# Cross-attention kernel: the first steps of each quad of heads in another order

## What is computed

```python
x = x + _L0_xattn_ref(_layernorm(x, axis=-1), ctx_2048, Wq, Wk, Wv, Wo)
# H, HD = 16, 128; 4096 keys
q = (inputs_q @ Wq).reshape(b, sq, H, HD) * (1.0 / np.sqrt(HD))
k = (inputs_kv @ Wk).reshape(b, skv, H, HD)
v = (inputs_kv @ Wv).reshape(b, skv, H, HD)
scores = jnp.einsum('bqhd,bkhd->bhqk', q, k)
attn = jax.nn.softmax(scores, axis=-1)
ctx = jnp.einsum('bhqk,bkhd->bqhd', attn, v).reshape(b, sq, H * HD)
return ctx @ Wo
```

## Time and profile before

| | |
|---|---|
| median of 3 runs | 1721.75 us (1721.35 to 1724.09) |
| profiled execution | 1724.57 us, span 1722.7 us |
| mean granted TensorE clock | 0.991 |
| TensorE busy | 1668.6 us, 97% |
| VectorE busy | 1090.3 us, 63% |
| ScalarE busy | 695.9 us, 40% |
| GpSimd busy | 99.0 us, 6% |

### The profile page before, as it was taken

How to read it: one execution, slowest core, us unless ns; L and a number is a source line. 1 busy time by engine, 2 the same in 40 slices (tenths; PEclk the granted TensorE clock), 3 DMA queues, 4 the chain that set the end, 5 groups by cost and what they waited for, 6 DMA issues and landing times.

```text
span 1722.7 us, 23442 instructions
## 1 busy us (share of the span) xinstructions
PE 1668.6 (97%) x9232; PEld 1307.9 (76%) x9232; DVE 1090.3 (63%) x1746; ACT 695.9 (40%) x938; POOL 99.0 (6%) x183
## 2 busy tenths in 40 slices
PE   8998999999999999999999999998899999999998
PEld 7887888888788888788888888887658556544444
DVE  4445777776777777767777788895555805433333
ACT  3334444454544444544445455554322312222221
POOL 0000000000000000000000000101000000000000
PEclk9999999999999999999999999999899999999999
DMA  6754544545445454544545433325111438388880
GB/s 220 215 164 147 135 128 135 134 128 138 133 128 132 129 139 120 148 127 129 137 122 141 129 111 92 96 88 196 75 49 40 182 123 350 90 336 328 322 327 32
DMA packets 114765, 262.54 MB, mean 152 GB/s; under 512 B 6688, under 2 KB 76512, under 8 KB 108512
## 3 DMA queue, kind: packets, MB, share of 16 engines
q1 hardware_dynamic: 96224, 193.93, 36.4%
q0 software_dynamic: 18432, 67.12, 13.1%
HBM read 193.35 MB, written 67.67 MB: 152 GB/s over the span
## 4 chain that ended last, share of the span: by engine, by line
PE 72%; issue 18%; DVE 4%; DMA 2%; POOL 2%; ACT 2%; SPq 0%; DVEq 0%; POOLq 0%; ACTq 0%
PE bank L41 17%; PE bank L390 16%; PE bank L362 12%; PE bank L403 7%; PE bank L1882 5%; PE bank L1551 3%; PE bank L1903 2%; PE bank L1902 2%; PE bank L1911 2%; DMA v_dram<-v_out 1%; POOL v_back L887 1%; PE bank L428 1%; PE bank L135 1%; DMA v_out<-in_wv 1%; PE bank L1096 1%
## 5 line engine op out<-in xcount | busy, mean ns | idle before, releaser
L716 DVE TENSOR_TENSOR e_lo<-S,e_hi 128x1024 fp32r<-128x1024 f32 x128 | 156.6, 1223 | 89.2 <-ACT e_hi L548 88.8
L362 PE MATMUL bank<-cT_hi,wk_hi 128*128 128x512 f32 x512 | 205.3, 401 | 0.0
L390 PE MATMUL bank<-wv_hi,cT_hi 128*128 128x512 f32 x512 | 199.8, 390 | 3.5 <-DVE wv_lo L653 3.5
L362 PE MATMUL bank<-cT_hi,wk_lo 128*128 128x512 f32 x512 | 200.5, 392 | 0.0
L539 ACT ACTIVATE S<-S 128x1024 f32<-128x1024 f32 x128 | 135.8, 1061 | 159.0 <-DVE S L696 158.8
L390 PE MATMUL bank<-wv_hi,cT_lo 128*128 128x512 f32 x512 | 199.5, 390 | 0.0
L362 PE MATMUL bank<-cT_lo,wk_hi 128*128 128x512 f32 x512 | 199.2, 389 | 0.0
L390 PE MATMUL bank<-wv_lo,cT_hi 128*128 128x512 f32 x512 | 199.2, 389 | 0.0
L548 ACT CAST e_hi<-S 128x1024 fp32r<-128x1024 f32 x128 | 135.0, 1055 | 145.7 <-PE bank L403 141.7
L709 DVE TENSOR_TENSOR esum<-esum,S 128x512 f32<-128x512 f32 x210 | 145.0, 690 | 72.0 <-ACT S L539 68.4
L403 PE MATMUL bank<-e_hi,v_back 128*128 128x256 f32 x880 | 167.3, 288 | 9.3 <-DVE small L734 4.6
(11 more groups left out here) (271 smaller groups left out, 2838.0 us busy)
## 6 DMA issues: line engine op xcount, KB each, us to landing
w<-in_w_moe SPq DMA_DIRECT2D x32, 2304.0 KB, 8.5
v_dram<-v_out SPq DMA_DIRECT2D x112, 512.0 KB, 4.6
v_back<-v_dram POOLq DMA_DIRECT2D x110, 512.0 KB, 4.9
v_dram<-v_back SPq DMA_DIRECT2D x16, 512.0 KB, 3.9
ctx_nat<-in_ctx SPq DMA_DIRECT2D x8, 1024.0 KB, 4.9
ctx_raw<-in_ctxT SPq DMA_DIRECT2D x7, 1024.0 KB, 8.1
v_late<-v_dram POOLq DMA_DIRECT2D x14, 512.0 KB, 3.5
l_w_qkv<-in_l_wqkv SPq DMA_DIRECT2D x6, 1024.0 KB, 7.6
```

What stands on the lines that cost most here:

```text
L362: t = e.matmul(banks[b][:], l, r, start=(c == 0 and m == 0), stop=(c == DT - 1 and m == 2))
L390: t = e.matmul(banks[b][:], l, r, start=(c == 0 and m == 0), stop=(c == DT - 1 and m == 2))
L716: e.tensor_tensor(lo[:], Sj, hi[:].bitcast(F32), ALU.subtract).then_inc(e_split, 1)
```

## The change

Three things are put elsewhere at the start of each quad (heads 0, 4 and 8), with no work added or taken away.

- Values: the units of the next quad start with step 2, which has two (0 and 1); steps 3 to 5 have one each (2, 3, 4), step 6 two (5 and 6), from step 7 on it is as before. Unit 31 of the first quad goes from the end of the opening stage into step 0 of head 0, between keys and scores; its store goes behind the loads of weight pieces 0 and 1 in SP's queue.
- Weights: rounding and splitting of the four pieces are put behind the rounding, raising and splitting of scores in steps 0 and 1. In step 1 ACT stores scores and does step 1's rounding and step 2's raising ahead of pieces 2 and 3. On DVE `split_k` comes ahead of `sum_e` in step 1, and `add_head` behind everything else.
- Head closing: in step 0 of heads 4 and 8 `finish_head` comes ahead of `scores`, and DVE's `invert_sum` ahead of the sums.

```diff
@@ units
-            return [] if s == 0 else [first, first + 1] if s == 1 else [first + s]
+            if s < 2:
+                return []
+            return [first + u for u in ((0, 1) if s == 2 else (5, 6) if s == 6 else (s - 1,) if s < 6 else (s,))]
+
+        def starts_quad(h):
+
+            return h < LATE and h % HPQ == 0
@@ sync_cross
-                for u in range(CT * j, CT * (j + 1)):
+                for u in range(CT * j, min(CT * (j + 1), KVT - 1)):
                     spill(u)
...
                                 load_wv(h // HPQ + 1, c)
+                                if h == 0 and c == 1:
+                                    spill(KVT - 1)
@@ tensor_cross
-                for u in range(CT * j + (1 if j else 0), CT * (j + 1)):
+                for u in range(CT * j + (1 if j else 0), min(CT * (j + 1), KVT - 1)):
                     project_v(u)
...
                     for u in units(h, j):
                         project_v(u)
+                    if j == 0 and h == 0:
+                        project_v(KVT - 1)
+                    if j == 0 and h and starts_quad(h):
+                        finish_head(h - 1)
                     scores(h + 1, j)
-                    if j == 0 and h:
+                    if j == 0 and h and not starts_quad(h):
                         finish_head(h - 1)
@@ scalar_cross, step 0 and step 1
                         round_k(h + 1, 0)
+                        if h == 0:
+                            round_v(KVT - 1)
                         for u in units(h, 0):
                             round_v(u)
                         raise_scores(h, 0)
-                        if h % HPQ == 0:
+                        round_e(h, 0)
+                        raise_scores(h, 1)
+                        if starts_quad(h):
                             round_wv(h // HPQ + 1, 0)
                             round_wv(h // HPQ + 1, 1)
-                        round_e(h, 0)
-                        raise_scores(h, 1)
                         continue
                     if j == 1:
                         round_k(h + 1, 1)
-                        if h % HPQ == 0:
-                            round_wv(h // HPQ + 1, 2)
-                            round_wv(h // HPQ + 1, 3)
+                    if j == 1 and starts_quad(h):
+                        store_scores(h + 1, 0)
+                        round_e(h, 1)
+                        raise_scores(h, 2)
+                        round_wv(h // HPQ + 1, 2)
+                        round_wv(h // HPQ + 1, 3)
+                        continue
@@ vector_cross, step 0 and step 1
                         shift(h, 0)
+                        if h == 0:
+                            split_v(KVT - 1)
                         for u in units(h, 0):
                             split_v(u)
                         shift(h, 1)
-                        if h % HPQ == 0:
+                        if h and starts_quad(h):
+                            invert_sum(h - 1)
+                        sum_e(h, 0)
+                        split_e(h, 0)
+                        if starts_quad(h):
                             split_wv(h // HPQ + 1, 0)
                             split_wv(h // HPQ + 1, 1)
-                        sum_e(h, 0)
-                        split_e(h, 0)
-                        if h:
+                        elif h:
                             invert_sum(h - 1)
                         continue
                     if j == 1:
-                        if h:
+                        if h and not starts_quad(h):
                             add_head(h - 1)
-                        sum_e(h, 1)
-                        split_k(h + 1, 1)
-                        if h % HPQ == 0:
-                            split_wv(h // HPQ + 1, 2)
-                            split_wv(h // HPQ + 1, 3)
+                        if starts_quad(h):
+                            split_k(h + 1, 1)
+                            sum_e(h, 1)
+                        else:
+                            sum_e(h, 1)
+                            split_k(h + 1, 1)
                         shift(h, 2)
                     split_e(h, j)
                     keep_max(h + 1, j - 1)
+                    if j == 1 and starts_quad(h):
+                        split_wv(h // HPQ + 1, 2)
+                        split_wv(h // HPQ + 1, 3)
+                        if h:
+                            add_head(h - 1)
```

More of the change, by code:

```diff
@@ L583, in scalar_cross @@
                 round_v(CT * j + 2)
-                round_v(CT * j + 3)
+                if j + 1 < NCH:
+                    round_v(CT * j + 3)
             for h in range(LATE):
@@ L769, in vector_cross @@
                 split_v(CT * j + 2)
-                split_v(CT * j + 3)
+                if j + 1 < NCH:
+                    split_v(CT * j + 3)
             for h in range(LATE):
```

## The result

| | before | after |
|---|---|---|
| median | 1722.92 us (4 runs, 1721.35 to 1724.41) | 1737.27 us (4 runs, 1736.0 to 1739.76) |
| ratio, 95% interval | | 1.0085 [1.0068, 1.0103] |
| profiled execution, mean clock | 1724.57 us, 0.991 | 1739.76 us, 0.986 |

The changed kernel is slower by 14.35 us (11.7 to 17.7 by the interval). The forecast was +8.5, with a range that ended at 1735.0: the direction was right, the size was not.

A forecast was written before the change was run, and what follows sets the result against it. TensorE, busy 97% of the span, was taken as the bound; idle time at the quad starts changes by 4.35 + 2.2 + 1.95 = +8.5 us, giving 1730.3 against the median 1721.75, with 8 in 10 within 1722.5 to 1735.

The forecast's parts named there:

- the closing in the hole of `k_lo`: Step 0 of heads 4 and 8: closing, 1.77 us long, fills the wait before the scores; 1.40 us removed.
- the first weighing of heads 4 and 8 without a wait: `e_lo` ends at 435.62, so the first weighing starts at 435.67 without a wait.
- `wv_lo` no longer late: Second quad: the 0.89 us wait for `wv_lo` is removed, as the last split ends before the first value set.
- the scores of step 1: Second quad: TensorE leaves weighing at 437.17 and waits for the stored bank until 437.94, 0.6 us idle.
- The walk along DVE: Second quad: DVE has the sums pair and a shift in front of weighing 1's `e_lo`, which ends at 441.38.
- the landing of the reloads: `v_back` reloads land 3.45 us after issue behind a quiet queue; the first quad's first reload takes 3.85.
- The clock: Rival, chance 0.22: one to three further falls to half clock, up to 1.7 us each; +10.2 to +13.6 in all.
- holes of 2.5 and 2.25 us: TensorE idles 2.5 us before weighing 1 of the first quad, 2.25 at step 2's pair in each later quad.
- The pair at step 2: ACT waits for the first unit's store before rounding the second; TensorE idles 2.25 us, 0.8 in the first quad.
- 1.8 + 2.25: Second quad: 1.8 us idle before weighing 1, starting at 441.44, plus 2.25 at the pair of step 2.
- 8.36 instead of 6.1 and 1.35 instead of 2.5: First quad: 6.1 us idle before weighing 0 for the late first reload, then 2.5 before weighing 1.
- A side sum: By the skill page's transfer estimate, reloads come 0.25 to 0.6 us earlier and the sum is about 1.5 us smaller.

The follow-up runs named there:

- kernel 6: The changed kernel, with loads of weight pieces 2 and 3, and what follows them on SP, held until the reload has landed: 1754.4 us, 1.0171.
- kernel 10: The changed kernel, with idle matmuls put into the holes before weighing 0 and 1 of head 0 and weighing 1 of heads 4 and 8: 1737.43 us, 1.0073.
- kernel 5: The changed kernel, with the keys of step 2 put ahead of weighing 1 at heads 0, 4 and 8: 1745.84 us, 1.0122.
- 14: The changed kernel, with the second unit of both pairs rounded and split behind the next step's key work: 1735.75 us, 1.0071.
- 4: The kernel before, with unit 31 of the first quad and its store moved as in the change, nothing else: 1728.21 us, 1.0023.
- 7: The changed kernel, with unit 31 and its store back where they were before: 1734.34 us, 1.0054.
- 2: The kernel before, with head closing and the reciprocal ahead of scores at heads 4 and 8 alone: 1723.88 us, 0.9998.
- 11: The changed kernel, with head closing behind scores again at heads 4 and 8: 1741.57 us, 1.0092.
- 1: The kernel before, with the values' order alone changed (none in step 1, pairs in steps 2 and 6): 1738.28 us, 1.0081.
- 3: The kernel before, with the weight pieces behind the raised scores alone, values still in step 1: 1731.16 us, 1.0038.
- Kernel 12: The run with scores of step 1 ahead of the values kept there, with the pair's second unit put off behind step 2's key work: 1717.61 us, 0.9963.
- 13: The kernel before, with the second unit of step 1's pair rounded and split behind step 2's keys: 1722.79 us, 0.9988.
- 9: Closing and weights as in the change; unit 31 and step 1's values as before, scores of step 1 ahead of those values: 1727.37 us, 1.0018.
- 15: The changed kernel with step 2's keys ahead of weighing 1, and the second unit of both pairs put off: 1734.69 us, 1.0062.

## Why the prediction fell short

**Right.** The direction; the places of all holes; the closing in the hole of `k_lo`; the first weighing of heads 4 and 8 without a wait; `wv_lo` no longer late; 0.48 at the scores of step 1 (0.6 forecast). The walk along DVE, which went through a dozen instructions, forecast the end of `e_lo` of weighing 1 for 441.38. DVE's timeline of the new trace has it at 450.13, which is 441.4 in old times:

```profile
448.91 1.22 DVE L735 TENSOR_TENSOR e_lo<-S,e_hi 128x1024 fp32r<-128x1024 f32 x1
```

**The sum against the traces.** TensorE's waits of 0.3 us and more in the three quads add up to 12.7 us before and 21.8 after. That is 9.0 us more, where the sum has 8.5. TensorE's work at 0.50 grew from 2.9 to 11.75 us, which costs up to half of the difference, 4.4 us; the sum has nothing for it. Together this makes up to 13.4 us, against 12.95 measured. So the idle time came out nearly right in total, by errors that cancel, and most of what the sum lacks is the granted clock.

**The step that failed: the landing of the reloads, and the half clock behind their holes, put at nothing.** "[L]ands 3.4 to 5.6 us later; I take 3.45 behind a quiet queue". The queue isn't quiet: the change itself puts the reload next to pieces 2 and 3, and in the second quad next to `wq` as well. It took 5.7 us there, against 3.45, and 3.8 when the loads were held (kernel 6). So the reload and not `e_lo` releases weighing 1, at 452.19, which is 443.5 in old times against 441.44. In the first quad the store was issued at 143.0 in old times, as forecast, but took 5.15 instead of 4.6 and the reload 5.5 instead of 3.85: weighing starts at 154.04 in old times, not 151.8. The rows had a landing of 5.6, but it was used for stores alone in the range. The walk itself held the warning: it splits pieces 0 and 1 until 437.1, which frees SP to load 2 and 3, and issues the reload at 437.6. The Trainium skill, page "DMA: Bandwidth & Descriptors", section "Issuing engines are not separate DMA queues", says that the engines which issue transfers share the same 16 DMA engines; kernel 6 fits this, with 3.8 us against 5.7 for a reload that POOL issues beside SP's loads. Which of the three loads beside it matters most wasn't run.

**The clock was a rival and came in each quad.** Of further falls the sum has none; the rival, at 0.22, expected them behind holes of 2.5 and 2.25 us and forecast +10.2 to +13.6, which holds the 12.95 of the traces. With the reloads at 5.7 us the holes were of 3.9 and 4.0, near the 3.93 behind which the old trace shows one already. In the second quad the idle time is as forecast, and the growth is +3.6 instead of +2.2; 3.41 us at half rate account for up to 1.7. The price of a fall depends on what sets the pace behind it: kernel 10 removed all of them and won some 2 us of at most 5.9, within the noise, while in kernel 5 TensorE set the pace behind the hole and 5.8 us of work at 0.50 made three sets 2.6 us longer.

**A term that shrank.** The pair at step 2 was priced at 2.25 us; it shows 0.49. From landing to scores it takes the 4.8 us of the walk. But TensorE was ready 3.8 us later than the walk had it, after the longer hole and the half clock, and `k_lo` only 1.9 us later. In old times the scores of step 3 start at 463.8 in after, 464.3 in kernel 10 and 463.3 in kernel 5, while TensorE was ready at 463.3, 462.6 and 458.6: hence waits of 0.49, 1.76 and 4.68, and none when the second unit is put off (14). So 1.8 + 2.25 became 3.90 + 0.49, and the second quad's idle time, 5.51, agrees with the forecast 5.5 by luck, two errors that cancel. In the first quad 8.36 instead of 6.1 and 1.35 instead of 2.5 cancel in part as well.

**A side sum.** Reloads that land 0.25 to 0.6 us earlier would not make the sum "about 1.5 us smaller": by the walk only the two reloads of the first quad set a start, and `e_lo` sets the others, so it would be under 1 us. Nothing rests on it.

**The shares.** Unit 31: 4 to 5 us (4, 7). Closing: 0 to 1 us in its favour (2, 11). Values: 14 alone (1), weights 6.5 alone (3), and the four together also 14, not 24.5. The two large parts overlap: with the values gone from step 1 nobody waits for late weights, so the 3.38 of kernel 3 falls away in the change. How much either would cost with everything else in place wasn't run. Nor is the late landing the whole of it: kernel 1 loses 14 us with a reload of 3.65, because the values no longer lie over what TensorE then waits for.

**What was in it.** Closing and weights in the new places, with the values left in step 1, can give a gain, which the change gave up by taking the values out of the gap between two reloads, and by the late store of unit 31. Kernel 12 keeps the values there, in the shadow of the reload, and takes ACT's wait for the store out of the way; it also has the scores of step 1 ahead of the values, which the change has not. Of its 6.4 us some 2 come from putting off alone (13); the rest appears only with both edits, since 9 alone is about 3 us slower than before. From 9 to 12 one edit wins 0.55%; what vanished is the wait of 3.14 us, and the half clock behind it.

## What to carry to other kernels

Price a moved transfer by rows with the same neighbours on all queues, and work out first which loads the new order issues beside it. With a single buffer, count the work between its release and its next use: if that is shorter than the round trip, the work in the gap was the cover, and moving it away costs what it hid. When a hole grows near the size behind which the old trace shows a clock fall, put the fall into the sum and not among the rivals. On an engine that works in order, put an instruction that waits for a transfer behind what the bottleneck engine needs next. And when one wait changes size, work out the later ones again, since a later wait shrinks by what TensorE has already lost.

## What the runs showed of the hardware

- A reload of 512 KB, DRAM to SBUF, took 3.5 to 4.0 us at the three places in kernel 6 where the loads were held back. With both weight pieces issued in the 1.6 us ahead of it (512 KB, with `wq` 768) it took 4.97 to 6.50 us, in 23 cases in the traces of after and of kernels 5, 7 to 10, 12, 14 and 15. A store of 512 KB took 3.86 us, 5.05 with a reload issued 0.3 us behind it (kernel 5), and 6.12 with one issued 0.4 us ahead of it (kernel 6).
- At the quads' starts, over all traces, the granted clock stayed at 1.00 behind every hole of 0.6 to 1.76 us. From 1.80 to 3.61 us it went both ways: 0.50 behind 1.80 (kernel 15, third quad) and 1.99 (kernel 6), 1.00 behind 2.75 (kernel 11), 3.12 (kernel 9) and 3.61 (kernel 2). Above that it was 0.50 each time, for 3.41 us, or 6.83 and 10.24 around longer holes. Such a stretch can begin inside the hole: around the 8.36 us it lasted 10.24 us, 4.6 of them before TensorE had work.
- Keeping the full clock by idle matmuls through the holes returned only about 2 us, within the noise, of the up to 5.9 that 11.75 us of work at half rate could have cost; the other engines set the pace behind the holes.
